# Row numbers for the padding slots of a graph kernel's gathers: spread over the table in place of row 0

## The chip, the cores and the metric

One core of one Trainium2 chip. The metric is the time of one execution on the device in microseconds (us), the median of several. Shares of TensorE's clock are of its full speed.

## What is computed

Four graph layers, one after the other, on 6250 nodes of 256 float32 features and one list of 100000 edges (src, dst, two kinds of edge type), sorted by dst. Each layer adds up, for every node, what its edges bring from their source nodes. Cut to the parts that gather:

```
# L0: agg = segment_sum(h[src], dst); conv = agg @ wr.T + br + h @ wroot.T; gelu, batch norm, + x
# L1: three times:
xr  = einsum('nd,rde->rne', x, W_rel[l])              # 8 relations
agg = segment_sum(xr[edge_type_8, src], dst)
x   = relu(agg + x @ W_root[l] + bias[l])
# L2: messages of src and of 16 relation vectors, summed by dst, into a GRU cell
# L3: attention with 4 heads:
e   = leaky_relu(a_src[src] + a_dst[dst], 0.2)
alpha = softmax of e over the edges of a dst
out = segment_sum(h[src] * alpha, dst) + bias
# each block is followed by normalisation and a residual sum
```

## The kernel before

**Buckets, chunks and slots.** The nodes are cut into 49 buckets of 128 rows (`NT`). A bucket's edges are packed into chunks of 128 slots, one slot per partition, and each bucket begins a new chunk. The program has room for 832 chunks (`NCH`), 106496 slots; the buckets lie in order of their number of chunks. Counted from the inputs, 807 chunks hold edges. The 6496 slots without an edge are padding: 3176 of them lie at the ends of the last chunks of 48 buckets (2 to 127 in one), 120 in chunk 806, the last one with edges, and 3200 are the whole of chunks 807 to 831, which the program adds to the last bucket.

**Six passes.** `gathers` (L716 to L722, GpSimd's queue) walks through the 832 chunks five times: order 0 reads rows of the input `in_x`, orders 1 to 3 read `rel_d` (8 relations x 6272 rows of 1 KB, so 1 KB per slot) and order 4 reads `rows_d`. A sixth pass (L742) reads rows of 1064 bytes from `att_d`. Each gather is one indirect DMA: for chunk c, partition p gets row `edges[p, word, c]` of the table, 128 rows in all. Up to 16 gathers of orders 0 to 4 may be ahead of the sums (`U`), and 5 groups of 8 chunks in the last pass (`GBUF`).

**Sums.** For each chunk VectorE writes a 128x128 one-hot matrix of the slots' destinations (L1771) and TensorE multiplies it with the gathered rows (`sum_chunk`, L1112); VectorE adds the product to the bucket's tile (L1788). A padding slot has an all-zero row in the one-hot, so whatever it gathers is multiplied by 0. Between the sums TensorE does the dense work of buckets that are complete (L1334 for `rel_d`, for instance). The last bucket is complete only with chunk 831, and the next order's first gather waits until all buckets' rows are written back.

**Where the row numbers come from.** In the first 560 us the edges are sorted on the chip. Each edge's two words are routed to its slot, half through matmuls into PSUM (`route`, L1158 and L1160) and half through scatters to `slots_d` (L707), which SyncE loads back. An empty slot reads 0. At the end VectorE adds the two halves (`routed`, L1694), shifts out the low bits (L1696), and L1699 subtracts `LEAST` and clips at 0, so that every padding slot gets row 0. The row numbers of `rel_d` are made from it later (L1721). The first gather waits for L1699.

**Around it in the preparation.** GpSimd's order is the scatters L707, an iota L711 (49x832), the memset L714 of half of the sums' tile (6528 words per partition), then the gathers. VectorE's order at this place is the one-hots L1654 and L1655, three small operations, the copies L1679 and L1680 out of PSUM, L1683 twice, L1687, then `routed`. The tile `g` (`gflat`) is free for other uses until the first gather, once the last slots are routed.

The two lines that make the row number:

```
routed(0)
dve.tensor_scalar(edges[:, 0, :], word_i[0], -float(LEAST), 0.0, ALU.add, ALU.max).then_inc(s_prep_dve, 1)
```

Of the kernel before, what the change touches and what calls it, by code (L numbers as in the profile page):

```python
# [21 lines left out]
ALU = mybir.AluOpType  # L22
# [3 lines left out]
P = 128  # L26
N, D, E = 6250, 256, 100000
# [7 lines left out]
NSB = -(-(EC + 1) // SB)  # L35
# [3 lines left out]
ROUTES = 6  # L39
# [9 lines left out]
NCH = CI * U  # L49
# [11 lines left out]
MANT, LEAST = 13, 113 * 1024  # L61
# [15 lines left out]
NPH = 8  # L77


READY = 4  # L80
READY0 = 4
assert 0 < ETAIL <= 32 and EC % NG >= max(POOL_G) and EC // NG == TB - 1
assert max(N, P << LOW_BITS) <= 30 * 1024 and LEAST % (1 << LOW_BITS) == 0
assert NT == TU * TI and NCH == U * CI and U == 2 * GR and NCH % GR == 0
assert all(U * min(t + READY, CI) * NT >= (t + 1) * NCH for t in range(NT)) and CI - READY <= NT

# [5 lines left out]
PREP_DVE = {n: k + 1 for k, n in enumerate([  # L92
    "base", "bound", "marks", "bucket", "src", "planes", "w1s", "cvec", "y_free", "diag0"])}
# [33 lines left out]
def program(nc, a, out):  # L127
    ctx = ExitStack()
    with ctx:
        def sb(name, shape, dt=F32):  # L130
            return ctx.enter_context(nc.sbuf_tensor(name, shape, dt))

        def sem(name):
            return ctx.enter_context(nc.semaphore(name))
# [20 lines left out]
        edges = sb("edges", [P, 4, NCH], I32)  # L155
        edges_f = edges[:, :, :].bitcast(F32)
        g = sb("g", [P, U, D + R2])
        gflat = g[:, :, :].rearrange("p u d -> p (u d)")
# [23 lines left out]
        word_i = [v.bitcast(I32) for v in word_f]  # L182
# [19 lines left out]
        slot_col = eflat[:, e0:e0 + NCH]  # L202
        assert e0 + NCH <= 8 * NCH
        blank = gflat[:, 0:NCH]
        chunk_no = gflat[:, NCH:2 * NCH]
        word0, word1, word2 = (gflat[:, 2 * NCH + k * EP:2 * NCH + (k + 1) * EP] for k in range(3))
        int0, int1 = word0.bitcast(I32), word1.bitcast(I32)
# [149 lines left out]
        s_prep_dve = sem("s_prep_dve")  # L357
# [16 lines left out]
        s_sort = sem("s_sort")  # L374
# [2 lines left out]
        s_sc = [sem(f"s_sc{k}") for k in range(max(POOL_G))]  # L377
        s_loaded = sem("s_loaded")
        s_chunk_no = sem("s_chunk_no")
        s_zero = sem("s_zero")  # L380
        s_conv = sem("s_conv")
        s_gelu = sem("s_gelu")
# [109 lines left out]
        per_sb, half_sb = len(sort_cols), (0, NG - POOL_G[0], len(sort_cols))  # L492
# [15 lines left out]

        def beside_sweep(eng, trip, dense, ready=READY):


            for i in range(0, ready):
                trip(i, None, None)
            trip(ready, 0, None)
            for i in range(ready + 1, CI):
                trip(i, i - ready, i - ready - 1)
            for v in range(CI - ready, NT + 1):
                dense(v if v < NT else None, v - 1)

        def beside_gru(eng, trip, hook):  # L520


            for i in range(0, READY):
                trip(i, None, None, None)
            trip(READY, 0, None, None)
            trip(READY + 1, 1, 0, None)
            for i in range(READY + 2, CI):
                trip(i, i - READY, i - READY - 1, i - READY - 2)
# [152 lines left out]
        def _(pool):  # L681
# [3 lines left out]
                      allow_small_or_imprecise_dtypes=True).then_inc(s_const, 1)  # L685
            pool.iota(prow, pattern=[[1, 1]], base=0, channel_multiplier=1,
                      allow_small_or_imprecise_dtypes=True).then_inc(s_const, 1)
# [5 lines left out]
                      allow_small_or_imprecise_dtypes=True).then_inc(s_const, 1)  # L693
            pool.memset(zrow, 0.0).then_inc(s_const, 1)
            pool.iota(chunk_no, pattern=[[1, NCH]], base=0, channel_multiplier=0,
                      allow_small_or_imprecise_dtypes=True).then_inc(s_const, 1)

            pool.wait_ge(s_blank_d, 16)
            for t in range(TB):
                if t % 2 == 0:  # L700
                    pool.wait_ge(s_slots, t // 2 + 1)
                for k in range(POOL_G[t % 2]):
                    before_t = sum(k < POOL_G[u % 2] for u in range(t))
                    if before_t:
# [5 lines left out]
            pool.wait_ge(s_read, TB)  # L710
            pool.iota(count_m[:, 0, :], pattern=[[1, NCH]], base=0, channel_multiplier=0,  # L711
                      allow_small_or_imprecise_dtypes=True).then_inc(s_chunk_no, 1)
            pool.wait_ge(s_rank, TB)
            pool.memset(A[:, 0:NT // 2, :], 0.0).then_inc(s_zero, 1)  # L714

# [829 lines left out]
        def _(dve):  # L1545
            link = Link(dve, s_dve)
# [149 lines left out]
                link(dve.tensor_scalar(word_i[w], word_i[w], MANT, None, ALU.logical_shift_right))  # L1696

            routed(0)
            dve.tensor_scalar(edges[:, 0, :], word_i[0], -float(LEAST), 0.0, ALU.add, ALU.max).then_inc(s_prep_dve, 1)  # L1699
            routed(1)  # L1700
            link(dve.tensor_scalar(word_i[2], word_i[1], LOW_BITS, None, ALU.logical_shift_right))
            link(dve.tensor_scalar(edges_f[:, 2, :], word_i[2], -float(LEAST >> LOW_BITS), None, ALU.add))
# [540 lines left out]
```

## Time and profile before

| what | value |
|---|---|
| median of 3 runs | 7747.83 us (7735.52, 7747.83, 7780.11) |
| profiled execution, its own time | 7759.3 us |
| its span, first to last instruction | 7757.3 us |
| mean granted TensorE clock | 0.907 |
| busy: TensorE, VectorE, ScalarE, GpSimd | 81%, 62%, 32%, 65% |
| GpSimd's gathers | 832 x 6, some 0.95 us each |

Two phases matter for reading it. Up to about 563 us the edges are sorted; from there on each order takes about 1050 us, with dense stages between some of them, and the attention pass runs from 6352 us to about 7580 us. A share of busy time is a mean over all of these. "DMA to landing" is the time from the start of an issue to the arrival of its last byte. "issue" as a releaser means that the engine waited for nothing that the trace shows.

### The profile page before, as it was taken

What the parts mean: (1) busy time and instruction counts of PE and PEld (TensorE: products, weight loads), DVE (VectorE), ACT (ScalarE), POOL (GpSimd) and SP (SyncE); (2) the same over time, 40 slices, a digit from 0 to 9 for tenths busy, and PEclk for the clock granted to TensorE, in tenths of its full rate; (3) what the DMA queues carried; (4) which work ended last, traced back from release to release, by engine and by line L of the source; (5) the groups of instructions that cost most, each with busy time, mean ns of one, the idle gap of its engine ahead of it and who ended that gap; (6) DMA issues with size and microseconds to landing.
All of it is one profiled execution on the core that took longest, in us unless ns stands there. A gap on an engine that the chain in (4) does not pass through costs nothing.

```text
span 7757.3 us, 105260 instructions
## 1 busy us (share of the span) xinstructions
PE 6270.8 (81%) x25864; PEld 3867.7 (50%) x25864; DVE 4847.9 (62%) x16599; ACT 2447.4 (32%) x7538; POOL 5056.3 (65%) x5303
## 2 busy tenths in 40 slices
PE   8987888889888888888887666668888868888880
PEld 5545555544455554444444444444555546666660
DVE  7986555545455554444444555545777768878878
ACT  3651111112111111011112222221222227777766
POOL 3657777720477776777776777767777757666650
PEclk9998988889899999899998778877999989989995
DMA  1004333344455556455556777773333456666662
GB/s 58 3 20 130 105 105 105 105 89 151 138 159 157 157 158 137 135 157 158 157 158 180 247 240 243 243 215 114 112 111 111 112 106 219 221 199 212 214 181 66
DMA packets 559179, 1141.73 MB, mean 147 GB/s; under 512 B 111895, under 2 KB 304380, under 8 KB 558462
## 3 DMA queue, kind: packets, MB, share of 16 engines
q0 software_dynamic: 249024, 659.51, 32.4%
q1 hardware_dynamic: 195886, 366.27, 13.3%
q10 hardware_dynamic: 113680, 109.21, 4.1%
q8 instruction: 233, 3.82, 0.2%
q14 instruction: 356, 2.92, 0.1%
HBM read 822.31 MB, written 312.26 MB: 146 GB/s over the span
## 4 chain that ended last, share of the span: by engine, by line
PE 37%; POOL 20%; DMA 18%; issue 12%; DVE 11%; ACT 1%; DVEq 1%; ACTq 0%; SPq 0%; POOLq 0%
POOL g L722 20%; PE ps L1112 13%; DMA g<-rel_d,edges 9%; DMA wt<-turned_d 7%; PE ps L1304 4%; PE ps L1334 3%; PE ps L1524 2%; PE ps L1510 2%; DMA g<-rows_d,edges 2%; DVE AY L1788 2%; PE ps L1495 2%; DVE edges L1655 1%; PE ps L1500 1%; DVE edges L1654 1%; PE ps L1158 1%
## 5 line engine op out<-in xcount | busy, mean ns | idle before, releaser
L722 POOL DMA_INDIRECT g<-rel_d,edges x2496 | 2373.1, 951 | 1231.9 <-issue 649.9
L1788 DVE TENSOR_TENSOR AY<-AY,ps 128x256 f32 (+1 forms) x4160 | 1741.4, 419 | 2279.0 <-PE ps L1112 2261.1
L1112 PE MATMUL ps<-g,rows 128*128 128x256 f32 (+1 forms) x4160 | 1403.8, 438 | 690.9 <-DMA g<-rel_d,edges 243.1
L1112 PE MATMUL ps<-g,oh 128*128 128x256 f32 (+1 forms) x4160 | 1449.8, 454 | 295.8 <-DVE rows L1771 95.7
L1112 PEld LDWEIGHTS ps<-g,rows 128*128 128x128 f32 x4160 | 732.7, 206 | 1296.9 <-issue 574.1
L1112 PEld LDWEIGHTS ps<-g,oh 128*128 128x128 f32 x4160 | 799.1, 219 | 749.4 <-issue 375.8
L722 POOL DMA_INDIRECT g<-rows_d,edges x832 | 798.5, 960 | 280.0 <-issue 221.9
L722 POOL DMA_INDIRECT g<-in_x,edges x832 | 797.2, 958 | 273.9 <-issue 193.0
L1334 PE MATMUL ps<-AY,turned 128*128 128x512 f32 x1568 | 755.1, 605 | 0.9 <-ACT turned L749 0.9
L749 ACT ACTIVATE wt<-ps 128x512 f32<-128x512 f32 (+1 forms) x448 | 250.1, 559 | 1463.0 <-PE ps L1334 1428.3
L2061 DVE TENSOR_REDUCE AY<-ps 128x4 f32<-128x512 f32 x832 | 569.1, 684 | 159.1 <-PE ps L1500 156.6
L1771 DVE TENSOR_SCALAR rows<-col,edges 128x128 f32<-128x128 f32 x2080 | 623.5, 300 | 37.9 <-issue 24.9
L1771 DVE TENSOR_SCALAR oh<-col,edges 128x128 f32<-128x128 f32 x2080 | 630.1, 303 | 23.4 <-DMA marks_d<-oh 18.0
L742 POOL DMA_INDIRECT g<-att_d,edges x336 | 318.6, 948 | 210.4 <-PE ps L1524 91.8
L707 POOL DMA_INDIRECT slots_d<-AY,g x294 | 288.9, 983 | 243.2 <-DVE g L1645 167.2
L749 ACT ACTIVATE AY<-ps 128x512 f32<-128x512 f32 (+3 forms) x421 | 181.3, 445 | 821.4 <-PE ps L1409 783.3
L1495 PE MATMUL ps<-AY,big_ident 128*128 128x512 bf16 x832 | 332.5, 400 | 133.2 <-DMA wt<-turned_d 128.4
L742 POOL DMA_INDIRECT AY<-att_d,edges x336 | 318.6, 948 | 161.8 <-PE ps L1524 99.9
L1334 PEld LDWEIGHTS ps<-AY,turned 128*128 128x128 f32 x1568 | 304.9, 195 | 220.2 <-issue 197.7
L1500 PEld LDWEIGHTS ps<-AY 96*128 96x128 bf16 x3328 | 269.1, 101 | 203.3 <-issue 31.4
L2074 DVE TENSOR_TENSOR AY<-AY,ps 128x260 f32 x832 | 345.8, 416 | 7.2 <-PE ps L1524 5.9
L1304 PE MATMUL ps<-AY,turned 128*128 128x512 f32 x784 | 347.2, 596 | 0.0
(384 smaller groups left out, 9687.2 us busy)
## 6 DMA issues: line engine op xcount, KB each, us to landing
rel_d<-wt ACTq DMA_DIRECT2D x392, 256.0 KB, 2.4
turned_d<-AY SPq DMA_DIRECT2D x104, 512.0 KB
wt<-turned_d SPq DMA_DIRECT2D x104, 512.0 KB
AY<-marks_d SPq DMA_DIRECT2D x104, 512.0 KB
rel_d<-g SPq DMA_DIRECT2D x49, 1024.0 KB, 4.4
g<-rel_d,edges POOLq DMA_INDIRECT x2496, 3.0
marks_d<-oh SPq DMA_DIRECT2D x104, 256.0 KB
marks_d<-rows SPq DMA_DIRECT2D x104, 256.0 KB
```

Of the source, the lines that this page charges most:

```text
L722: pool.indirect_dma_start(out=g[:, j, 0:width], out_offset=None, in_=table, in_offset=bass.IndirectOffsetOnAxis(ap=edges[:, word, c:c + 1] ...
L742: pool.indirect_dma_start(out=group_at(k)[:, j, 0:W4], out_offset=None, in_=att_d, in_offset=bass.IndirectOffsetOnAxis(ap=edges[:, 0, c:c ...
L749: return act.activation(o, v, ACT.Copy)
L1112: ins = pe.matmul(sum_slot(order, j), one_hot_at(j % OHS), g[:, j, 0:width], start=True, stop=True)
L1304: ins = pe.matmul(ps[:, q, :], turned[:, b, k * P:(k + 1) * P], relations[0][:, k, q * 512:(q + 1) * 512], start=(k == 0), stop=(k == KD - 1))
L1334: ins = pe.matmul(ps[:, 4 + q % 2, :], turned[:, 0, k * P:(k + 1) * P], w[:, k, q * 512:(q + 1) * 512], start=(k == 0), stop=(k == KD - 1))
L1495: pe.matmul(o.rearrange("p (h e) -> p h e", h=H), big_ident[:, :], miss[:, k % 2, P * j:P * (j + 1)].rearrange("p (o e) -> p o e", o=1).br ...
L1500: ins = pe.matmul(o[:, h * P:(h + 1) * P], pick[:, at:at + 1].broadcast_to([kr, P]), spread_t[:, k % 2, :], start=False, stop=(h == H - 1) ...
L1771: dve.tensor_scalar(one_hot_at(j % OHS), col[:, :], edges_f[:, 2, k:k + 1], None, ALU.is_equal)\
L1788: dve.tensor_tensor(tile_at(A, t, width), tile_at(A, t, width), sum_slot(order, j), ALU.add)\
L2061: dve.tensor_reduce(red[:, c % REDS, :], ps[:, SP_BANKS[c % len(SP_BANKS)], :].rearrange("p (h e) -> p h e", h=H), AX, ALU.max)\
L2074: dve.tensor_tensor(tile_at(A, t, W3), tile_at(A, t, W3), ps[:, WT_BANKS[c % len(WT_BANKS)], 0:W3], ALU.add)\
```

## The change

`filler` is a table [128, 832] in the free part of `g`: partition p, chunk c holds c + 42 p, at most 6165, below the 6250 rows of the smallest table. GpSimd writes it with one iota after L711, behind two waits: for VectorE's three small operations ("bound") and for the last routing matmul. VectorE then multiplies it by (word is 0), so that it stays only at padding slots, and takes the greater of it and word - `LEAST`. What the padding slots gather is multiplied by 0 as before.

```diff
+FILL_STEP = (N - NCH) // P
...
+        filler = gflat[:, 0:NCH]
...
             pool.iota(count_m[:, 0, :], pattern=[[1, NCH]], base=0, channel_multiplier=0,
                       allow_small_or_imprecise_dtypes=True).then_inc(s_chunk_no, 1)
+            pool.wait_ge(s_prep_dve, PREP_DVE["bound"])
+            pool.wait_ge(s_sort, ROUTES + per_sb * NSB)
+            pool.iota(filler, pattern=[[1, NCH]], base=0, channel_multiplier=FILL_STEP,
+                      allow_small_or_imprecise_dtypes=True).then_inc(s_filler, 1)
             pool.wait_ge(s_rank, TB)
             pool.memset(A[:, 0:NT // 2, :], 0.0).then_inc(s_zero, 1)
...
             routed(0)
-            dve.tensor_scalar(edges[:, 0, :], word_i[0], -float(LEAST), 0.0, ALU.add, ALU.max).then_inc(s_prep_dve, 1)
+            dve.wait_ge(s_filler, 1)
+            link(dve.scalar_tensor_tensor(filler, word_i[0], 0.0, filler, ALU.is_equal, ALU.mult))
+            dve.scalar_tensor_tensor(edges[:, 0, :], word_i[0], -float(LEAST), filler, ALU.add, ALU.max)\
+                .then_inc(s_prep_dve, 1)
             routed(1)
```

GpSimd's order between the last scatter and the first gathers, before:

```order
L707 DMA slots_d<-AY,g 106496x4 [waits s_sc2]
L711 IOTA AY 49x832 [waits s_read]
L714 MEMSET AY 128x6528 [waits s_rank]
L722 DMA g<-in_x,edges 128x256 [waits s_prep_dve]
L722 DMA g<-in_x,edges 128x256 x15
```

and in the changed kernel, whose lines are numbered 3 to 7 higher here:

```order
L710 DMA slots_d<-AY,g 106496x4 [waits s_sc2]
L714 IOTA AY 49x832 [waits s_read]
L718 IOTA g 128x832 [waits s_sort,s_prep_dve]
L721 MEMSET AY 128x6528 [waits s_rank]
L729 DMA g<-in_x,edges 128x256 [waits s_prep_dve]
L729 DMA g<-in_x,edges 128x256 x15
```

The memset now stands behind a wait for the last routing matmul; before, it waited only for `s_rank` and `s_read`, which are done earlier.

VectorE's order at the end of the preparation, before:

```order
L1679 COPY small<-ps 49x1 [waits s_prep_pe]
L1680 COPY small<-ps 49x1
L1683 TENSOR_SCALAR AY<-AY,small 49x832 [waits s_chunk_no,s_dve]
L1683 TENSOR_SCALAR AY<-AY,small 49x832
L1687 CAST bucket_of<-ps 1x512 [waits s_prep_pe]
L1687 CAST bucket_of<-ps 1x320
L1694 TENSOR_TENSOR AY<-AY,ps 128x512 [waits s_sort,s_loaded]
L1694 TENSOR_TENSOR AY<-AY,ps 128x320
L1696 TENSOR_SCALAR AY<-AY 128x832 [waits s_dve]
L1699 TENSOR_SCALAR edges<-AY 128x832 [waits s_dve]
L1694 TENSOR_TENSOR AY<-AY,ps 128x512
```

and in the changed kernel, from the first of the two 49x832 operations on:

```order
L1690 TENSOR_SCALAR AY<-AY,small 49x832 [waits s_chunk_no,s_dve]
L1690 TENSOR_SCALAR AY<-AY,small 49x832
L1694 CAST bucket_of<-ps 1x512 [waits s_prep_pe]
L1694 CAST bucket_of<-ps 1x320
L1701 TENSOR_TENSOR AY<-AY,ps 128x512 [waits s_sort,s_loaded]
L1701 TENSOR_TENSOR AY<-AY,ps 128x320
L1703 TENSOR_SCALAR AY<-AY 128x832 [waits s_dve]
L1707 SCALAR_TENSOR_TENSOR g<-AY,g 128x832 [waits s_filler,s_dve]
L1708 SCALAR_TENSOR_TENSOR edges<-AY,g 128x832 [waits s_dve]
L1701 TENSOR_TENSOR AY<-AY,ps 128x512
```

One operation of 832 elements has become two of another kind, and a wait for the iota stands ahead of them. Everything else on the five engines keeps its place.

## Rows read from the trace of the kernel before

**Rows 1.** The page: the chain of work that ended last, by line.
```profile
POOL g L722 20%; PE ps L1112 13%; DMA g<-rel_d,edges 9%; DMA wt<-turned_d 7%; PE ps L1304 4%; PE ps L1334 3%; PE ps L1524 2%; PE ps L1510 2%; DMA g<-rows_d,edges 2%; DVE AY L1788 2%; PE ps L1495 2%; DVE edges L1655 1%; PE ps L1500 1%; DVE edges L1654 1%; PE ps L1158 1%
```

**Rows 2.** The gathers of L722, 2100 to 2900 us: count, ns min/median/max, starts, landing.
```profile
L722 POOL DMA_INDIRECT g<-rel_d,edges x638: 942/949/1020, 2099.5 to 2898.9; - x160
...
DMA to landing us min/median/max: 2.7/2.8/4.8
```

**Rows 3.** The chain in order of time: start, us, what; ends of orders 1 to 4.
```profile
3061.99 16.85 DMA g<-rel_d,edges
3078.98 1.19 PE ps L1112 x2
...
4139.63 16.05 DMA g<-rel_d,edges
...
5217.45 20.38 DMA g<-rel_d,edges
...
6295.97 14.83 DMA g<-rows_d,edges
```

**Rows 4.** The last 19 gathers of order 0, as in rows 2.
```profile
L722 POOL DMA_INDIRECT g<-in_x,edges x19: 945/949/986, 1589.9 to 1612.5; - x19
...
DMA to landing us min/median/max: 7.2/11.2/14.0
```

**Rows 5.** Windows: us; busy PE, PEld, DVE, ACT, POOL; PEclk, DMA share, GB/s.
```profile
2900.00:3030.00 130.00, 113.27 (x387) 66.64 (x386) 66.32 (x221) 25.97 (x52) 98.49 (x104) 1.00 0.54 159
3040.00:3079.70 39.70, 27.64 (x83) 15.82 (x82) 13.24 (x42) 5.18 (x10) 17.46 (x19) 0.90 0.98 103
4118.00:4156.50 38.50, 28.54 (x76) 15.02 (x75) 12.29 (x40) 4.38 (x8) 17.09 (x19) 0.85 0.85 105
5195.00:5239.00 44.00, 33.26 (x71) 17.14 (x71) 14.75 (x52) 5.41 (x9) 17.91 (x19) 0.50 0.97 139
6280.00:6311.60 31.60, 25.24 (x73) 14.05 (x71) 16.24 (x59) 8.07 (x17) 12.96 (x14) 0.79 0.94 78
1600.00:1627.40 27.40, 19.60 (x63) 12.40 (x64) 10.56 (x39) 3.06 (x9) 10.41 (x11) 0.82 0.92 75
```

**Rows 6.** The chain at the end of the attention pass.
```profile
7470.83 5.49 DMA wt<-turned_d
...
7481.56 7.14 DMA wt<-turned_d
...
7510.05 11.50 DMA wt<-turned_d
...
7528.80 7.62 DMA wt<-turned_d
```

**Rows 7.** Windows of the attention pass, columns as in rows 5: middle, slow stretch.
```profile
6850.00:6960.00 110.00, 97.29 (x606) 71.24 (x604) 81.81 (x283) 71.07 (x309) 63.90 (x68) 0.83 0.59 185
6700.00:6810.00 110.00, 98.53 (x745) 72.64 (x746) 99.19 (x342) 86.28 (x377) 78.23 (x83) 1.00 0.71 227
```

**Rows 8.** GpSimd's timeline: start, us, what [idle before, releaser].
```profile
536.02 0.84 POOL L711 IOTA AY<- 49x832 f32 x1
536.79 5.55 POOL L714 MEMSET AY<- 128x6528 f32 x1
562.95 0.99 POOL L722 DMA_INDIRECT g<-in_x,edges  x1 [20.61 <-DVE edges L1699]
```

**Rows 9.** VectorE's timeline, same columns.
```profile
535.53 7.08 DVE L1655 TENSOR_SCALAR edges<-edges,g 128x832 f16<-128x832 f16 x1
...
542.69 0.42 DVE L1655 TENSOR_SCALAR edges<-edges,g 128x832 f16<-128x832 f16 x1
...
589.02 1.03 DVE L1721 SCALAR_TENSOR_TENSOR edges<-AY 128x832 int32<-128x832 f32 x1
```

**Rows 10.** The chain at the end of the preparation.
```profile
550.41 0.86 PE ps L1166 x4
...
552.98 1.34 DVE AY L1683 x2
...
562.08 0.59 DVE edges L1699
```

More of the change, by code:

```diff
@@ L379, in program @@
         s_chunk_no = sem("s_chunk_no")
+        s_filler = sem("s_filler")
         s_zero = sem("s_zero")
```

## The prediction

> **What bounds the kernel now.** I began with the chain of work that ended last. Its largest part is GpSimd issuing gathers, then sums on TensorE, and 11% of the span are landings of gathers from rel_d and rows_d [rows 1]. So next: how a gather behaves in the middle of an order. In 800 us of order 1, 638 gathers start 1.255 us apart (2898.9 less 2099.5, over 637) and land 2.8 us after their start in the median, 4.8 at most [rows 2]. The order runs at GpSimd's pace; transfers follow it with room to spare, at a DMA share of 0.54 [rows 5].
>
> The chain in order of time shows what differs at the ends. The last gather of orders 1, 2, 3 and 4 takes 16.85, 16.05, 20.38 and 14.83 us to land, the next piece in the chain is the sum that waited for it (at 3078.98 in order 1), and nothing can follow, because only this sum completes the last bucket [rows 3]. Order 0 shows the same: its last 19 gathers land after 7.2 to 14.0 us [rows 4]. The windows say of what kind the delay is. In the ends the DMA engines are busy for 0.85 to 0.98 of the time and yet move 75 to 139 GB/s in all, where at 0.54 they moved 159 [rows 5]. Packets are in the engines and take long; it is not that too many bytes are asked for.
>
> What is particular to these gathers is in the program: chunks 807 to 831 are all padding and chunk 806 nearly (120 of 128), so 26 gathers in a row read one and the same row 128 times each. The backlog gives their price. It grew by 14.0 us (16.85 less 2.8) over 26 gathers, 0.54 us each on top of the pace of 1.255: some 1.8 us for a gather that should need less than 1.25. The other orders give 1.7 to 1.9.
>
> **The change, part by part.** First the ends of orders 0 to 4. If 128 different rows cost what they cost in rows 2, the last gather lands after 2.8 us and no backlog forms. From rows 3 and 4 this takes off 14.0 - 2.8 = 11.2 us in order 0, 14.05 in order 1, 13.25 in order 2, 17.6 in order 3 and 12.0 in order 4: **68 us**, the upper end. The lower end is TensorE's own work in these stretches, which must still be done: window less busy time leaves 7.8, 12.1, 10.0, 10.7 and 6.4 us, **47 us** together [rows 5]. That end is too low: busy time there holds waits within a pipelined pair and much of it ran at a clock of 0.50 to 0.90, which idling had brought down, while in the steady stretch at clock 1.00 TensorE was busy for 113.27 us in 104 gathers, 1.09 us each and below the pace [rows 5]. Only order 3 is doubtful; its whole end ran at 0.50 (1.2 GHz). I take **60 us**, nearer to the upper end, since four of five ends can be kept at GpSimd's pace.
>
> Second, the end of the attention pass. There TensorE waits once per group of 8 chunks for a one-hot that SyncE loads, and the same DMA engines carry the gathers. A group takes 10.7 us (7470.83 to 7481.56); the last ones take 28.5 us for two and 18.75 us for one, with landings of 11.50 and 7.62 us in place of 5.49 [rows 6]. That is 7.2 and 8.1 us above the steady step. The first part begins with a landing of 7.14 us before the padded gathers are under way, so it need not be theirs. The bounds are 0 and 15.3; I take **8 us**, the second step.
>
> Third, the preparation. The memset on GpSimd (5.55 us) and VectorE stand in each other's way: beside iota and memset one L1655 takes 7.08 us where the next takes 0.42 [rows 8, 9], and everything behind it, the last routing matmuls too, waits. The changed kernel moves the memset behind these matmuls. They then end 5.55 us earlier, at 550.4 - 5.55 = 544.9 us (the chain leaves them at 550.41 [rows 10]). The new iota takes as long as L711, 0.84 us, and the memset then holds GpSimd until 551.2. L1683 (552.98 before, 547.4 now) falls into this. If it is held like L1655 it starts at 551.2, 1.8 us earlier than before; if not, 5.55 us earlier. On top come two new operations of 832 elements for one: 1.03 us each (L1721 is the same kind and size [rows 9]) plus the step between them, less the 0.59 of L1699 [rows 10], +1.5 us. The wait for the filler costs nothing in either case, since the iota ends long before L1696; without the memset's removal ahead of it, it would cost the iota's 0.84. So the first gather starts 0.3 us earlier if L1683 is held, and 4 us earlier if it is not; if something else holds the chain, such as the load from slots_d, it is 1.5 us later. L1655 is the nearest row, so I take **0.3 us**. L1679 and L1680 read PSUM and no row shows such an operation beside a memset.
>
> The Trainium skill (SBUF — State Buffer, Who interferes with whom) says that VectorE and GpSimd share one port pair, held for a whole instruction, but only by VectorE's two-port modes or by its second SBUF input against a GpSimd read. By that rule L1683 is held and the copies from PSUM are not, which is the case above; the two new operations would not be held by a memset even if they met it.
>
> Everything else costs nothing: the filler lies in space that is free, the one-hots and sums are the same, and the number of gathers and bytes is the same.
>
> The sum: 60 + 8 + 0.3 = 68.3 us off the profiled execution's own 7759.3 is 7691.0. That execution stands 11.5 us above the median of the runs shown, so against the median the forecast is 7747.8 - 68.3 = **7679 us**, 0.9% faster. A measurement of this kernel can tell about 0.5%, 39 us, from no change.
>
> **The rivals.**
>
> *TensorE takes the place of the transfers.* In order 3's end it was busy 33.26 us for 24 gathers, 1.39 each, at clock 0.50, above the pace of 1.255 [rows 5]. If the clock stays low in all ends and the attention pass gives nothing, the lower end holds: 47 us, **7701**. For it: the clock of 0.50. Against it: the other orders ran at 0.79 or more even while waiting. Chance 0.13.
>
> *More than the ends.* 23 chunks in the second half of each order have 75 or more padding slots too, and the attention pass has stretches such as 6850 to 6960 us, with 68 gathers in 110 us at clock 0.83, where another takes 83 at clock 1.00 [rows 7]. If a late one-hot behind half-padded gathers sets these off, one such stretch is worth 15 gathers of 1.33 us, 20 us, and two may go: 68 + 40 off, **7640**. Against it: in the middle of orders such gathers land within 4.8 us [rows 2], hidden by 16 gathers of lead. Chance 0.12.
>
> *The change doesn't do what it says.* The ends might be slow for another reason (25 chunks in a row into one bucket, for instance, on VectorE or TensorE). Then it is **7748**. Against it: VectorE is busy 13.24 of 39.70 us there, and the DMA share is 0.98 [rows 5]. Chance 0.04.
>
> *Slower: an even pitch collides in memory.* The place of row 0 is taken by rows 42 KB apart over the partitions. If such rows fall on few memory channels, these 26 gathers get slower than now, in all six passes. The point of decision is the present 1.8 us per gather: at 2.1 us the loss is 26 x 0.3 x 5 = 39 us, and at 3.0 us it is 26 x 1.2 x 5 = 156, **7904**. For it, no row of this trace; against it, 42 KB is no power of two and scattered rows of edges run well. Chance 0.03.
>
> The Trainium skill (DMA: Bandwidth & Descriptors, Latency and other measured facts) has such a case: copies with a row pitch of 2 MiB ran at 164 GB/s and of 4 MiB at 103, against 207 at 512 KiB, and 4 KiB of extra pitch restored the rate. It lists none near 42 KB. By that rule this change is safe; nothing it states on one row read many times bears on the gain.
>
> **How the numbers follow.** The forecast case has the remaining 0.68. Its own range is 47 to 84 us off (68 + 15.3 + 0.3 at the upper end): 7664 to 7701, wider by some 8 us each way for the spread of the runs (7735 to 7780). To leave out no more than 2 in 10 the range takes in the first rival and half of the second: **7648 to 7708**. Faster by over 0.5% means under 7709: all but a little of the forecast case, the second rival, and four fifths of the first, 0.65 + 0.12 + 0.10 = 0.87. Within 0.5%: 0.10. Slower by over 0.5%: 0.03.
>
> **What would show it.** In the changed kernel the last gathers of orders 0 to 4 should land within some 3 to 5 us, and the DMA share in the ends should fall to about the 0.5 to 0.7 of the stretch before, at 140 GB/s or more. The long L1655 should shrink to about 1.5 us, a long L1683 may show up instead, and the first gather should start at 559 to 563 us. Between the first gathers of two orders there should be 11 to 18 us less than before. The prediction is wrong if the last gathers still land after 10 us or more, or if they land early and TensorE's last sum still comes late.

## The result and the profile after

The changed kernel takes 7644.4 us (median of 4 runs, 7636.8 to 7659.9) against 7741.7 us before (4 runs): a ratio of 0.9871, 95% interval 0.9845 to 0.9896, or 97 us less. The forecast was 7679 us with a range from 7648 to 7708. The direction came out as forecast, and so did the mechanism at the ends of the orders; the size was too small by 29 us (97 against 68), and the time lies 4 us under the range. (The median of before had moved from 7747.8 to 7741.7 with its fourth run.)

The profiled executions differ by more, 7757.3 and 7647.9 us of span. The starts of the first and last gather of each pass say where the 109.4 us went:

| stretch | before, us | after, us | change |
|---|---|---|---|
| start to the first gather of order 0 | 563.0 | 562.2 | -0.8 |
| first to last gather, orders 0 to 4 together | 5230.7 | 5222.0 | -8.7 |
| last gather of order 0 to first of 1 | 406.7 | 393.7 | -13.0 |
| of 1 to 2 | 35.6 | 19.2 | -16.4 |
| of 2 to 3 | 32.5 | 19.3 | -13.2 |
| of 3 to 4 | 27.6 | 10.1 | -17.5 |
| of 4 to the attention pass | 56.4 | 44.8 | -11.6 |
| attention pass, first to last gather | 1175.4 | 1155.2 | -20.2 |
| last gather to the end | 229.5 | 221.4 | -8.1 |

Of the 28.3 us in the last two lines, most lie at one place. TensorE's attention pass has 104 groups of 8 chunks. From the start of the 98th group to the start of the 104th, the last, these rows give 86.5 us before and 63.6 us after, 22.9 less:

```profile
7465.64 0.39 PE L1495 MATMUL ps<-AY,big_ident 128*128 128x512 bf16 x1 [0.70 <-DMA wt<-turned_d]
...
7552.18 0.38 PE L1495 MATMUL ps<-AY,big_ident 128*128 128x512 bf16 x1
```

```profile
7379.47 0.39 PE L1502 MATMUL ps<-AY,big_ident 128*128 128x512 bf16 x1 [0.44 <-DMA wt<-turned_d]
...
7443.10 0.39 PE L1502 MATMUL ps<-AY,big_ident 128*128 128x512 bf16 x1 [0.57 <-DMA wt<-turned_d]
```

These six steps are used again below, as "the last six steps"; the stretch from the first gather of the pass to the 98th group is its "first part" (1113.3 us before, 1108.2 after).

The chain of work that ended last, by line, on the page after (its answer before is [rows 1]; L729 is the L722 of before, L1119 its L1112):

```profile
POOL g L729 18%; PE ps L1119 14%; DMA g<-rel_d,edges 9%; DMA wt<-turned_d 7%; PE ps L1311 4%; PE ps L1341 3%; PE ps L1531 2%; PE ps L1517 2%; DVE AY L1798 2%; PE ps L1502 1%; DMA g<-rows_d,edges 1%; DVE edges L1662 1%; PE ps L1507 1%; PE ps L1165 1%; DVE g L1780 1%
```

The shares have hardly moved; a percentage view does not show this change. The gathers of L729 do, over the whole execution (count, ns min/median/max, starts, then time to landing):

```profile
L729 POOL DMA_INDIRECT g<-rel_d,edges x2496: 940/946/1203, 2003.2 to 5167.0; - x192
L729 POOL DMA_INDIRECT g<-in_x,edges x832: 942/946/2397, 562.2 to 1609.4; - x167
L729 POOL DMA_INDIRECT g<-rows_d,edges x832: 942/946/1268, 5177.1 to 6226.5; - x167
...
DMA to landing us min/median/max: 2.6/2.8/8.3
```

The trace has the landing of 2080 of the 4160 gathers, and none of them takes longer than 8.3 us, where the last ones of the orders took 14 to 20 [rows 3, 4]. The chain in order of time at the end of order 1, after:

```profile
3043.91 2.77 DMA g<-rel_d,edges
...
3046.81 0.67 PE ps L1119 x2
3047.48 1.73 PE ps L1341 x4
```

and one row of before that answers to its last line:

```profile
3080.17 3.43 PE ps L1334 x4
```

The landing went from 16.85 to 2.77 us, 14.1 less. The same four matmuls behind the last sum take 1.73 us in place of 3.43: before, the granted clock was 0.50 there (3080.2 to 3083.6 us), after the wait. That is part of why this wait became 16.4 us shorter and not 14.1. The ends of orders 1 and 3 in windows (columns as in rows 5):

```profile
3022.00:3047.90 25.90, 23.43 (x83) 14.32 (x82) 13.55 (x43) 4.80 (x10) 17.37 (x19) 1.00 0.53 161
...
5143.00:5172.00 29.00, 19.79 (x71) 13.88 (x70) 15.30 (x54) 6.80 (x10) 19.17 (x20) 0.80 0.70 226
```

The DMA share fell from 0.98 to 0.53 and the rate rose from 103 to 161 GB/s in order 1, from 0.97 and 139 to 0.70 and 226 in order 3 [rows 5]. The clock rose from 0.90 to 1.00 and from 0.50 to 0.80. TensorE is busy for 23.4 of 25.9 us in order 1 and for 19.8 of 29.0 us in order 3: it fits under GpSimd's pace in both.

### The profile page after: what moved, and what is told of

It reads as the page before. It is cut to its first block, busy times and chain, and to the rows that moved or that the text cites. A ratio compares the mean times of both kernels' runs of the same rounds, so it can differ in the third digit from the quotient of the medians.

```text
span 7647.9 us, 105264 instructions
## 1 busy us (share of the span) xinstructions
PE 6216.9 (81%) x25864; PEld 3827.4 (50%) x25864; DVE 4850.1 (63%) x16600; ACT 2447.0 (32%) x7538; POOL 5046.7 (66%) x5304
## 4 chain that ended last, share of the span: by engine, by line
PE 39%; POOL 18%; DMA 18%; DVE 11%; issue 11%; ACT 1%; DVEq 1%; ACTq 0%; SPq 0%; POOLq 0%
POOL g L729 18%; PE ps L1119 14%; DMA g<-rel_d,edges 9%; DMA wt<-turned_d 7%; PE ps L1311 4%; PE ps L1341 3%; PE ps L1531 2%; PE ps L1517 2%; DVE AY L1798 2%; PE ps L1502 1%; DMA g<-rows_d,edges 1%; DVE edges L1662 1%; PE ps L1507 1%; PE ps L1165 1%; DVE g L1780 1%
## 5 line engine op out<-in xcount | busy, mean ns | idle before, releaser
L729 POOL DMA_INDIRECT g<-rel_d,edges x2496 | 2368.7, 949 | 1188.8 <-issue 637.9
L1798 DVE TENSOR_TENSOR AY<-AY,ps 128x256 f32 (+1 forms) x4160 | 1746.0, 420 | 2208.2 <-PE ps L1119 2192.7
L1119 PE MATMUL ps<-g,rows 128*128 128x256 f32 (+1 forms) x4160 | 1391.6, 434 | 674.4 <-DMA g<-rel_d,edges 228.3
L1119 PE MATMUL ps<-g,oh 128*128 128x256 f32 (+1 forms) x4160 | 1442.4, 452 | 270.5 <-DVE rows L1781 93.1
L1119 PEld LDWEIGHTS ps<-g,rows 128*128 128x128 f32 x4160 | 719.8, 203 | 1279.2 <-issue 537.3
L1119 PEld LDWEIGHTS ps<-g,oh 128*128 128x128 f32 x4160 | 796.3, 218 | 724.6 <-issue 366.3
L729 POOL DMA_INDIRECT g<-in_x,edges x832 | 795.1, 956 | 265.7 <-issue 183.4
L729 POOL DMA_INDIRECT g<-rows_d,edges x832 | 797.1, 958 | 262.4 <-issue 219.3
```

The source lines that it names most:

```text
L729: pool.indirect_dma_start(out=g[:, j, 0:width], out_offset=None, in_=table, in_offset=bass.IndirectOffsetOnAxis(ap=edges[:, word, c:c + 1] ...
L1119: ins = pe.matmul(sum_slot(order, j), one_hot_at(j % OHS), g[:, j, 0:width], start=True, stop=True)
L1798: dve.tensor_tensor(tile_at(A, t, width), tile_at(A, t, width), sum_slot(order, j), ALU.add)\
```

## The experiments

In all of them padding slots are still multiplied by zero, so none leaves out a part of the result. Each was timed beside runs of the kernel before on the same chip; "us under before" is against those runs. All diffs are against the changed kernel.

### Which padding slots count: `tail_only`, `partial_only`, `all_row0`, `after_again`

```diff
 # tail_only: row 0 before chunk 806, spread rows from there on
-            pool.iota(filler, pattern=[[1, NCH]], base=0, ...
+            pool.memset(filler[:, 0:806], 0.0).then_inc(s_filler, 1)
+            pool.iota(filler[:, 806:NCH], pattern=[[1, NCH - 806]], base=806, ...
 # partial_only: the reverse
+            pool.iota(filler[:, 0:806], pattern=[[1, 806]], base=0, ...
+            pool.memset(filler[:, 806:NCH], 0.0).then_inc(s_filler, 1)
 # all_row0: the whole mechanism, but row 0 for all
+            pool.memset(filler, 0.0).then_inc(s_filler, 1)
```

In the first two VectorE waits for both.

tail_only. 

> Only the padding slots of chunks 806 to 831 get spread rows; the 3176 padding slots at the ends of earlier buckets keep row 0. Theory A (the run of padded gathers at the end of each pass is all of the gain): faster than before by 90 us or more, the waits between the last gather of one order and the first of the next as short as with the whole change (18 to 28 us shorter than before is not needed, 11 to 18 us each is). Theory B (the earlier half-padded chunks give the unforeseen 20 us inside the attention pass): the waits between orders shrink as in the whole change, 72 us together, but the attention pass stays near 1175 us from first to last gather, and the time is 70 to 85 us under before.

partial_only. 

> The other half: only the 3176 padding slots before chunk 806 get spread rows, chunks 806 to 831 read row 0 throughout. Theory A: within 10 us of before. Theory B: 20 to 30 us faster than before, with the attention pass from first to last gather at about 1155 us; the last gathers of orders 0 to 4 land after 14 to 20 us as before in either case.

all_row0. 

> The whole change with a filler of zeros: the waits, the moved memset and the two new operations stay, every padding slot reads row 0. The sum of the prediction gives 0.3 us faster than before; if the preparation is worth anything, at most 4 us faster or 1.5 us slower. A difference of 20 us or more would say that moving the memset, and not the rows, moved the attention pass.

after_again. 

> The changed kernel once more, beside the others on one chip. About 100 us under before (0.987). If the attention pass is again 1155 us from first to last gather, its 20 us are of the change; if it lies anywhere from 1150 to 1175, they are what executions differ by.

Measured, with before at 7753.3 us:

| kernel | median, us | ratio to before, 95% interval |
|---|---|---|
| tail_only | 7673.7 | 0.9906 (0.9885 to 0.9928) |
| partial_only | 7746.3 | 0.9999 (0.9985 to 1.0013) |
| all_row0 | 7747.0 | 0.9999 (0.9986 to 1.0013) |
| after_again | 7657.4 | 0.9884 (0.9863 to 0.9905) |

`all_row0` settles one point: waits, moved memset and the two new operations are worth nothing that can be measured (the interval is 10 us either way). All the gain is the rows. `tail_only` holds most of it and stays 16 us behind the whole change, as its theory B said: the five waits between passes are 486.4 us together (558.8 before, 487.1 after), the attention pass is 1174.5 us, and the time is 80 us under before. `partial_only` alone gains nothing measurable, as its theory A said, and its last gathers of order 1 land as late as before:

```profile
L730 POOL DMA_INDIRECT g<-rel_d,edges x21: 942/946/972, 3031.8 to 3056.9; - x21
...
DMA to landing us min/median/max: 7.3/14.3/17.3
```

By these medians the earlier half-padded chunks (the last chunks of the buckets before chunk 806) are worth 16 us with the tail repaired and at most 7 us (7753.3 less 7746.3) with the tail as it was: the two don't add up, and the question was kept open. `after_again` had its attention pass at 1171.6 us in the profile, not 1155, so the 20.2 us of the table above are not all the change's. Its profiled execution was the slowest of its five, 14 us above their median.

### What about row 0 is slow: `row_of_chunk`, `same_each_chunk`, `pitch32`

```diff
 # row_of_chunk: row c for all partitions
-            pool.iota(filler, pattern=[[1, NCH]], base=0, channel_multiplier=FILL_STEP, ...
+            pool.iota(filler, pattern=[[1, NCH]], base=0, channel_multiplier=0, ...
 # same_each_chunk: row 42 p for all chunks
+            pool.iota(filler, pattern=[[0, NCH]], base=0, channel_multiplier=FILL_STEP, ...
 # pitch32: row c + 32 p
+            pool.iota(filler, pattern=[[1, NCH]], base=0, channel_multiplier=32, ...
```

row_of_chunk. 

> The filler is c alone (step 0 over the partitions): all padding slots of a chunk read one row, and the next chunk reads the next row. Theory A (what costs is one row asked for many times at once, within a gather): a padded gather still takes 1.5 us or more, the last gathers of orders 0 to 4 land after 8 us or more, and the time is within 40 us of before. Rival (what costs is that all gathers come back to the same row 0): landings of 3 us as in the changed kernel and 90 us or more under before.

same_each_chunk. 

> The filler is 42 p alone: 128 different rows within a gather, but the same 128 in each of the 26 padded gathers. Theory A: landings of about 3 us, time as in the changed kernel, 0.987 to 0.989 of before. Rival: slow like row 0.

pitch32. 

> The filler is c + 32 p: the rows of a gather lie 32 KB apart, a power of two, in place of 42 KB. If an even pitch collides in memory, the padded gathers take longer than 1.25 us, land late, and the time lies between the changed kernel and before, or above before at more than 1.8 us per gather. If not, it is the changed kernel's time within its noise, and the slower rival of the prediction has nothing behind it at this pitch.

Measured, with before at 7755.7 us: `row_of_chunk` 7702.1 (0.993, 0.9907 to 0.9953), `same_each_chunk` 7646.4 (0.9855, 0.9834 to 0.9875), `pitch32` 7642.7 (0.986, 0.9831 to 0.9889). The same 128 rows again and again are as good as new ones, so coming back to a row in the next gather costs nothing that can be measured. Rows 32 KB apart are as good as rows 42 KB apart, so the slower rival has nothing behind it at this pitch; other pitches were not tried.

`row_of_chunk` went against both readings. Theory A expected landings of 8 us or more and a time within 40 us of before, its rival 3 us and 90 us under before; measured are 4.2 us in the median and 54 us. The end of order 1 in its trace (gathers, landing, then a window):

```profile
L729 POOL DMA_INDIRECT g<-rel_d,edges x25: 942/946/989, 3015.3 to 3045.3; - x25
...
DMA to landing us min/median/max: 3.5/4.2/5.1
```

```profile
3015.00:3043.00 28.00, 23.30 (x81) 13.74 (x80) 13.69 (x46) 4.97 (x10) 21.04 (x23) 1.00 0.61 149
```

Landings of 3.5 to 5.1 us against 2.8 with spread rows show that one row per gather is slower by itself, but no backlog forms. What differs from row 0 is that the gathers in flight read different rows. A reading that fits all three kernels: requests for one row are served one after the other, at some 1.8 us for 128, and two rows are served side by side, so that gathers 1.25 us apart keep up when each has its own row. That the serving is by row, and where in the memory it happens, was not shown.

The DMA queue of the gathers gives their price more directly (packets, MB, share of 16 engines): the end of order 1 before (3063 to 3079 us), the stretch ahead of it (2900 to 3030 us), and `row_of_chunk` (3030 to 3047 us):

```profile
q0 software_dynamic: 416, 1.11, 89.6%
q0 software_dynamic: 4952, 13.52, 37.6%
q0 software_dynamic: 632, 1.72, 48.9%
```

For each MB the 16 engines are taken up for 12.9, 3.6 and 4.8 us. As an estimate from these rows, a gather of 128 x 1 KB takes all of them for 1.7 us with row 0, 0.5 us with the rows of edges, and 0.6 us with one row per gather. The first is above GpSimd's pace of 1.25 us and the others are below it, which fits that only row 0 leaves a backlog. The time of 7702 us was not explained by its profile, since the profiled execution was its fastest of six (7658 us; the others took 7666 to 7719); it was run again below.

### The preparation: `memset_later`

```diff
-            pool.wait_ge(s_rank, TB)
+            pool.wait_ge(s_prep_dve, PREP_DVE["marks"])
             pool.memset(A[:, 0:NT // 2, :], 0.0).then_inc(s_zero, 1)
```

memset_later. 

> The changed kernel, but the memset waits in addition until VectorE's two operations on 49x832 elements are done. In the changed kernel's trace these took 4.94 us beside the memset and 1.33 us in the trace of before. Expected: 1.3 us again, the first gather at 558.5 us in place of 562.2 to 563.0, and 3 to 4 us less in all, too little to be seen in the time. If the first gather stays at 562, something else holds the chain there, such as the load from slots_d.

First the timelines of the changed kernel itself, GpSimd and then VectorE:

```profile
543.32 0.83 POOL L718 IOTA g<- 128x832 f32 x1 [7.50 <-PE ps L1167]
544.08 5.54 POOL L721 MEMSET AY<- 128x6528 f32 x1
562.16 0.99 POOL L729 DMA_INDIRECT g<-in_x,edges  x1 [12.54 <-DVE edges L1708]
```

```profile
534.49 1.60 DVE L1662 TENSOR_SCALAR edges<-edges,g 128x832 f16<-128x832 f16 x1
...
545.49 0.15 DVE L1686 COPY small<-ps 49x1 f32<-49x1 f32 x1 [5.22 <-PE ps L1199]
545.57 0.14 DVE L1687 COPY small<-ps 49x1 f32<-49x1 f32 x1
545.74 4.94 DVE L1690 TENSOR_SCALAR AY<-AY,small 49x832 f32<-49x832 f32 x2
...
559.80 1.03 DVE L1707 SCALAR_TENSOR_TENSOR g<-AY,g 128x832 f32<-128x832 int32 x1
560.86 1.03 DVE L1708 SCALAR_TENSOR_TENSOR edges<-AY,g 128x832 int32<-128x832 int32 x1
```

The long operation moved as forecast: L1662 takes 1.60 us beside L714's iota where its counterpart took 7.08 [rows 9], and L1690 takes 4.94 us for its two, to 1.1 us after the memset's end, where they took 1.34 [rows 10]. The two copies out of PSUM take 0.15 us in the middle of the memset. In `memset_later` VectorE's pair is short again:

```profile
547.01 1.33 DVE L1690 TENSOR_SCALAR AY<-AY,small 49x832 f32<-49x832 f32 x2
```

```profile
557.60 0.99 POOL L729 DMA_INDIRECT g<-in_x,edges  x1 [3.66 <-DVE edges L1708]
```

The first gather starts at 557.6 us, 4.6 us before the changed kernel's and 0.9 earlier than expected. The memset is only half of it: the pair ends 2.3 us earlier, and the four matmuls between it and L1694 then take 3.6 us at a granted clock of 0.83, where they took 5.8 us at 0.50 in the changed kernel. In the time this is lost: 7664.7 us, 0.9882 (0.986 to 0.9905).

### The attention pass by itself, on a disturbed chip: `att_row0`, `att_only`, `tail_only_2`, `after_third`

```diff
 # att_row0: after the last sum of order 4, padding back to row 0
+            link(dve.tensor_copy(gflat[:, 0:NCH], edges[:, 0, :]))
+            dve.scalar_tensor_tensor(edges[:, 0, :], edges_f[:, 2, :], 0.0, gflat[:, 0:NCH], ALU.is_ge, ALU.mult)\
+                .then_inc(s_again, 1)
...
 # and before the attention pass's gathers
+            pool.wait_ge(s_again, 1)
```

`edges_f[:, 2, :]` is the slot's row within its bucket, negative for padding. `att_only` is `all_row0` with the same place used the other way round: GpSimd writes the table c + 42 p again, VectorE keeps it where that number is negative and takes the maximum. `tail_only_2` and `after_third` repeat kernels from above.

att_row0. 

> The changed kernel, but between order 4 and the attention pass VectorE sets all padding slots back to row 0 (two operations of 832 elements, 2 us at most, where GpSimd waits anyway). Only the attention pass sees row 0. Theory A (the attention pass gains from the spread rows, at its end about 15 us and on its way another 16): 25 to 35 us slower than the changed kernel beside it, so 60 to 75 us under before. Theory B (only its end gains, 15 us): 10 to 18 us slower than the changed kernel. The waits between orders 0 to 4 are short in both.

att_only. 

> The reverse: row 0 in orders 0 to 4, spread rows in the attention pass alone. Theory A: 25 to 35 us under before. Theory B: 10 to 18 us under before. The last gathers of orders 0 to 4 land after 14 to 20 us, as before.

tail_only_2. 

> Spread rows in chunks 806 to 831 alone, a second time, beside the changed kernel. First time it was 16 us slower than the changed kernel by the medians. Theory A: 10 to 20 us slower again, with the last steps of the attention pass near 10.7 us and long steps in its middle. Theory B: within 6 us of the changed kernel.

after_third. 

> The changed kernel, for the comparison of the three others on one chip: 0.987 to 0.989 of before.

On this chip before took 8803 us, and every kernel's time was 1050 to 1110 us longer than elsewhere. Two waits of `after_third`, and one of `after` for comparison (who <- by what: us, times, longest):

```profile
DVE AY L1798 <- remote: 1738.0, 392, 9.6
DVE AY L1798 <- PE ps L1119: 1048.7, 481, 14.2
```

```profile
DVE AY L1798 <- PE ps L1119: 2192.7, 1639, 14.3
```

Idle time is put down to something remote, which the traces of the other chips don't have. It need not be a cause: these traces also give no landing for any gather, so "remote" may stand for releases that could not be assigned, and `after` waits for 2192.7 us at the same line. Why the chip is slower is open; the granted clock was 0.83 to 0.84 in place of 0.91 to 0.92.

The medians are 8780.5 (`att_row0`), 8784.6, 8764.3 and 8767.5 us (`after_third`), the ratios 0.9976, 0.9978, 0.9953 and 0.9963 in the order above. `after_third` missed its expectation: the change is worth 0.4% here and not 1.2%. The gathers of order 1 start 1.44 us apart in place of 1.25 (1197.7 us over 831), not because an issue takes longer (0.95 us as elsewhere) but because GpSimd waits more often. At this pace little backlog can form: by the 1.8 us of a row-0 gather, 0.36 us times 26 is an estimated 9 us, not 14. The five waits between passes agree: 554.0 us with row 0 (`att_only`) and 524.9 us with different rows (`after_third`), 29 us apart where the pair of profiles of before and after has 72. `att_row0` was 13 us slower than `after_third` and `att_only` 18 us under before, which is near theory B's 10 to 18 us, and so is `tail_only_2`, 3 us faster than `after_third`; but with the whole change at 35 us they say little on the size elsewhere, and all were run again.

### The attention pass on a chip at the usual pace

att_row0_b. 

> Spread rows in orders 0 to 4, row 0 in the attention pass, again. Theory A (the attention pass gains at its end and on its way): 25 to 35 us slower than the changed kernel beside it. Theory B (only at its end): 10 to 18 us slower. In the profile, the last six steps of the attention pass take about 20 us more than six steps of 10.7 in either case.

att_only_b. 

> Row 0 in orders 0 to 4, spread rows in the attention pass alone, again. Theory A: 25 to 35 us under before. Theory B: 10 to 18 us under before. Last steps of the attention pass within 10 us of 10.7 each.

tail_only_c. 

> Spread rows in chunks 806 to 831 alone. Theory A: 10 to 20 us slower than the changed kernel beside it, as on the first chip. Theory B: within 6 us of it, as on the disturbed chip.

after_fourth. 

> The changed kernel beside the three others: 0.985 to 0.989 of before on a chip at the usual pace.

Measured, with before at 7755.6 us:

| kernel | median, us | ratio to before, 95% interval |
|---|---|---|
| att_row0_b | 7688.9 | 0.9915 (0.99 to 0.9929) |
| att_only_b | 7740.3 | 0.9978 (0.9966 to 0.9989) |
| tail_only_c | 7674.4 | 0.9893 (0.9874 to 0.9913) |
| after_fourth | 7663.5 | 0.9885 (0.9868 to 0.9901) |

The 92 us between before and `after_fourth` fall into 66.7 us for orders 0 to 4 (`att_row0_b` against before) and 25.4 us for the attention pass (`after_fourth` against `att_row0_b`). By `att_only_b` against before the attention pass is worth 15.4 us, on top of everything at row 0. So 15 to 25 us, the first in theory B's range and the second at the lower edge of theory A's; `tail_only_c`, 10.9 us slower than `after_fourth`, is in theory A's. Each interval is 9 to 13 us either way, so these shares are rough.

Its end is seen in the chain. `att_row0_b`, row 0 in this pass:

```profile
7408.66 6.06 DMA wt<-turned_d
...
7421.63 10.41 DMA wt<-turned_d
...
7439.08 5.82 DMA wt<-turned_d
...
7450.14 10.44 DMA wt<-turned_d
```

and `tail_only_c`, spread rows in the last chunks:

```profile
7448.14 5.82 DMA wt<-turned_d
...
7459.19 5.30 DMA wt<-turned_d
...
7469.73 4.78 DMA wt<-turned_d
```

With row 0 the loads of the one-hots take over 10 us twice, and two of the three steps are long, 13.0 and 17.5 us (the third is 11.1); with spread rows the load takes 4.8 to 5.8 us and the steps are 11.1 and 10.5 us.

The last six steps, measured as in the first section, separate the kernels without overlap:

| gathers of chunks 806 to 831 in the attention pass | kernels | last six steps, us |
|---|---|---|
| row 0 | before, `all_row0`, `partial_only`, `att_row0_b` | 86.5, 81.1, 84.2, 83.5 |
| different rows | ten profiles, from `after` to `tail_only_c` | 62.9 to 72.7, mean 66.3 |
| one row per gather | `row_of_chunk`, `row_of_chunk_b` | 74.3, 75.6 |

The end of the pass is worth 83.8 - 66.3 = 17.5 us. That was expected of `att_row0_b` (some 20 us over six steps of 10.7: 83.5 - 64.2 = 19.3) and of `att_only_b` (64.6 us, within 10).

The rest would be the earlier half-padded chunks. `tail_only` is 16.3 us slower than the changed kernel beside it on the first chip, 10.9 on this one and 3.2 us faster on the disturbed one. The first part of the pass, which holds none of the last six steps, takes 1110.2 to 1127.3 us in the five profiles with row 0 in these chunks, and 1087.3 to 1122.5 us in the nine with spread rows: means of 1119.3 and 1102.9, 16 us apart, in groups that overlap. The profile is one execution, and for two of the nine a fast one: `partial_only`'s was 16 us under its median and `att_only_b`'s, the fastest of ten, 25 us. The clock goes with it: it was 0.97 in the two shortest passes (1139.2 and 1140.8 us) and 0.93 in `tail_only`'s of 1174.5 us; which of the two sets the other was not shown.

Against it stands `partial_only`, whose pass was short in its profile and whose median over 12 runs did not gain, and `att_only_b`, whose 15.4 us are no more than the end alone. I take the effect of the half-padded chunks as likely, 10 to 16 us with the tail repaired, and not as settled. How it comes about was not shown either: long steps occur in the middle of the pass in every kernel.

### Two last runs: `row_of_chunk_b`, `memset_later_32`

The second is `memset_later` with the step of 32 rows.

row_of_chunk_b. 

> Row c for every padding slot of chunk c, again. Theory A (one row asked for 128 times is slow by itself, but two gathers in flight go to two rows and share the load, so that no backlog forms): landings at the ends of orders of 3.5 to 5 us, times of 7690 to 7710, as slow as spread rows in chunks 806 to 831 alone (7674) or slower because the attention pass still meets half-padded and padded gathers. Theory B (the first medians were chance): 7645 to 7665 like the changed kernel.

memset_later_32. 

> The changed kernel with the memset behind VectorE's two operations and a step of 32 rows. First gather at 557.6 to 558.5 us in place of 562 to 563, and 4 us less in all: 7640 to 7660, ratio 0.985 to 0.988, which can't be told from the changed kernel by its time.

Measured, with before at 7751.1 us: `row_of_chunk_b` 7673.0 (0.9906, 0.9888 to 0.9925), landings at the end of order 1 of 3.6 to 5.0 us; `memset_later_32` 7648.3 (0.9866, 0.9848 to 0.9883), first gather at 560.2 us. The landings are those of theory A; the time lies between its 7690 to 7710 and theory B's 7645 to 7665. One row per gather lands without a backlog again and loses 25 us against `memset_later_32` beside it. Its profiles show where some 16 us of this lie: the five waits between passes are 494.2 and 497.5 us together, where different rows have 486.4 to 489.9, and the last six steps are 8 to 9 us longer. The first part of its attention pass (1099.2 and 1104.0 us) is no longer than with spread rows, so one row in a half-padded chunk does no harm that is seen as long as the next chunk has another. Its first median of 7702 us, 29 above the second, stays unexplained.

The first gather of `memset_later_32` came later than the 557.6 to 558.5 us expected. VectorE's pair took 1.33 us there too, but the four matmuls behind it ran at a granted clock of 0.50, 5.8 us for `memset_later`'s 3.6. By its time `memset_later_32` cannot be told from the changed kernel, so no version beats it by a measurable amount.

## Why the prediction came out as it did

Direction and mechanism were right; two terms of the sum were too small and one effect stood at nothing.

**The ends of orders 0 to 4: mechanism right, term of 60 us too small.** By the times they gave 66.7 us (`att_row0_b` against before, 55 to 78 by its interval). By the profiles they gave more: the five waits between passes are 558.8 to 565.1 us together in four profiles with row 0 and 486.4 to 489.9 us in ten with different rows, 73 us apart in the mean. Both lie above the 60 us, against bounds of 47 and 68. The step that failed is the pull towards the lower end, which took TensorE's busy time during the wait for work that would stay. That busy time was itself stretched, by a clock of 0.90 and 0.50 in the ends of orders 1 and 3. With the wait gone the clock is 1.00 and 0.80 there, TensorE stays below GpSimd's pace, and the upper end holds; the clock gives a little on top, 1.7 us for four matmuls after order 1. The first rival, TensorE in place of the transfers, is refuted by the windows of orders 1 and 3.

**The end of the attention pass: term of 8 us, measured 17.5.** I took 15.3 us from three steps of the chain (by the rows it is 7.0 and 8.0, 15.1) as the upper bound and halved it, since the first of the long steps began before the padded gathers. Both parts of this failed. The rows end with the load for the last group but one, and the step from it to the last group took another 15.7 us (7536.46 to 7552.18), so that the last six steps were 22 us over 10.7 each and not 15; and the kernels with and without row 0 in these chunks differ by 17.5 us in the mean (81.1 to 86.5 against 62.9 to 72.7), so that nearly all of it was due.

**The half-padded chunks: put at nothing, with a chance of 0.12 for the rival of "more than the ends".** That may be right for orders 0 to 4, where the prediction's lead of 16 gathers hides them: from first to last gather the five orders take 5225.6 and 5232.5 us in the two `tail_only` profiles, beside 5219.4 to 5232.4 in the changed kernel and its equals. For the attention pass the two `tail_only` comparisons at the usual pace put it at 11 and 16 us, while `partial_only` and `att_only_b` show little or none. That the one-hots' loads share the DMA engines with the gathers, and so have no such lead, is the likely reason and was not tested. Of the 29 us missing, 7 to 13 belong to the first term and 9.5 to the second; the remaining 6 to 13 lie within this effect and the spread between sets of runs, and can't be told apart.

**The preparation: right in its parts, and nothing in the time.** The first gather starts 0.8 us earlier (0.3 forecast, 4 to -1.5 as bounds), which is less than the profiles of kernels with the same preparation differ by (562.2, 563.0 and 563.4 us for the changed kernel). Of the two cases the one with L1683 held came true, 4.94 us to just behind the end of the memset, and the two new operations took 1.03 us each, as priced by L1721. The pair ended 3.6 us earlier than before; the four matmuls behind it took 1.3 us more (clock 0.50 for 0.66) and the new operations 1.5, which leaves 0.8. By the Trainium skill's rule (SBUF — State Buffer, Who interferes with whom) the pair of tensor_scalar operations is held and copies from PSUM are not; the trace agrees with both, at 4.94 and 0.15 us. `all_row0` (0.9999) puts the whole part at nothing, give or take 10 us.

**That the change does what it says** was given 0.96, and `all_row0` against `after_again` shows it: 90 us by the row numbers alone. **Slower by an even pitch** was given 0.03; pitches of 32 and 42 KB are alike within the noise. The Trainium skill's rule on row pitches (DMA: Bandwidth & Descriptors, Latency and other measured facts) finds copies slower at pitches of 2 MiB and more, which no run here has.

**The range.** Its lower end took in half of the second rival, 7648. With the ends at 67, the attention pass at 25 and the preparation at nothing, the sum would have been 92 us off, 7656 against the median then shown, inside the range. That the measured 97 us lie outside it is in part chance: the changed kernel and the variants that equal it were 91 to 113 us under before in seven sets of runs at the usual pace, by the medians. Four of the seven medians (7648.3 to 7664.7 us) lie inside the range and three (7642.7 to 7646.4) under it. That the forecast of 68 us was too small is not chance: all seven lie above it.

## What to carry to other kernels

Slots that carry no work still cost transfers, and here, where they all named the same row, each gather of them took the DMA engines for more than three times as long as real work; a filler that differs from slot to slot cost one table and one more operation. Look for it where a run of such slots stands just before a point at which everything waits: there the backlog is fully exposed, while scattered ones hid behind the lead in orders 0 to 4. When a wait is to go away, don't bound the gain by an engine's busy time measured during the wait: its clock may be low there (0.79 to 0.90 in the ends of orders 1, 2 and 4 before [rows 5], 1.00 in the same places after). And when an upper bound is read from a chain, follow the chain to its last step.

## What the runs showed of the hardware

- A 128-row gather of 1 KB rows that all name one row takes an estimated 1.7 to 1.9 us in a run of such gathers, against a pace of 1.25 us that gathers of different rows keep without a backlog; the DMA engines show a share of 0.98 while moving 103 GB/s [rows 5].
- One row per gather, another in the next, is nearly as good as 128 different ones: landings of 3.5 to 5.1 us and no backlog. I had expected the repetition within a gather to decide.
- Such gathers slow the loads of another queue: beside them two 512 KB loads at the end of the attention pass of `att_row0_b` took 10.4 us, where they take 4.8 to 5.8 us beside spread rows (`tail_only_c`).
- A memset on GpSimd of 5.54 us holds a pair of float32 tensor_scalar operations of VectorE from SBUF to SBUF (4.94 us for 1.33) and leaves copies from PSUM alone (0.15 us).
- One chip ran all kernels at about 8800 us, for a reason that stays open; on it the change was worth 0.4%.
